# Causal softmax in chunks of 32 queries, its probabilities regrouped through DRAM

## The reference

```
x = _layernorm(x + _L0_attn_ref(x, wq, wk, wv, wo))
x = _layernorm(x + _L0_xattn_ref(x, ctx_4096, weight))
x = _layernorm(x + _L0_ffn_ref(x, A, B, Wr, br))
```

```
scores = jnp.einsum('bhqd,bhkd->bhqk', q, k) / math.sqrt(HEAD_DIM)
causal = k_pos <= q_pos
final = jnp.where(allowed, scores, NEG)
attn = jax.nn.softmax(final, axis=-1)
out = jnp.einsum('bhqk,bhkd->bhqd', attn, v)
```

## Time and profile before

| | |
|---|---|
| median of 3 runs | 1435.54 us |
| profiled execution | 1439.9 us |
| its span | 1438.1 us |
| TensorE busy | 1370.1 us, 95% |
| VectorE busy | 1092.5 us, 76% |
| ScalarE busy | 932.5 us, 65% |
| GpSimd busy | 985.9 us, 69% |
| DMA | 213.03 MB, mean 148 GB/s |

### The profile page before, as it was taken

One profiled execution on the slowest core, in us unless ns is written; L12 is line 12 of the kernel. 1 busy time (PEld: TensorE's weight loads), 2 busy tenths in 40 slices (PEclk: granted clock), 3 DMA queues, 4 the chain that ended last, 5 costly groups with the idle time before them and its releaser, 6 DMA issues. The chain is left out here.

```text
span 1438.1 us, 32297 instructions
## 1 busy us (share of the span) xinstructions
PE 1370.1 (95%) x8288; PEld 1061.4 (74%) x8288; DVE 1092.5 (76%) x3869; ACT 932.5 (65%) x3258; POOL 985.9 (69%) x936
## 2 busy tenths in 40 slices
PE   6899999999999999999985899999999999999995
PEld 4677777777777777777753688888888888888874
DVE  5677777777777777777766477878887788887784
ACT  5678878788787887878765354555554455555542
POOL 3677767777677776777754566777766777776753
PEclk9999999999999999999996899999999999999997
DMA  6345445454454544545465857656666766666751
GB/s 227 113 121 156 122 139 152 119 155 122 141 152 119 152 125 141 151 119 153 125 179 164 218 145 170 165 153 163 159 159 165 175 150 159 165 156 162 157 117 44
DMA packets 108861, 213.03 MB, mean 148 GB/s; under 512 B 26640, under 2 KB 32272, under 8 KB 108816
## 3 DMA queue, kind: packets, MB, share of 16 engines
q1 hardware_dynamic: 108816, 212.51, 54.0%
HBM read 131.83 MB, written 34.47 MB: 116 GB/s over the span
## 5 line engine op out<-in xcount | busy, mean ns | idle before, releaser
L432 PE MATMUL wo_ps<-weights,halves 128*128 128x512 f32 x2304 | 573.8, 400 | 11.9 <-DVE weights L611 11.8
L432 PEld LDWEIGHTS wo_ps<-weights,halves 128*128 128x128 f32 x2304 | 423.8, 189 | 129.3 <-issue 34.3
L694 ACT ACTIVATE pexp<-sm,smin 128x128 f32<-128x128 f32 x1024 | 398.7, 393 | 119.1 <-DVE smin L562 118.4
L1039 PE MATMUL wo_ps<-weights,halves 128*128 128x512 f32 x1488 | 401.1, 402 | 2.0 <-DVE yz L1142 2.0
L811 POOL TENSOR_TENSOR pn<-pexp,prec 128x512 f32<-128x512 f32 x256 | 267.8, 1046 | 151.6 <-DVE prec L569 151.5
L1392 POOL TENSOR_TENSOR prods<-prod,prods 128x512 fp32r<-128x512 f32 x192 | 259.9, 1362 | 134.0 <-ACT prods L1286 129.1
L1039 PEld LDWEIGHTS wo_ps<-weights,halves 128*128 128x128 f32 x1488 | 273.4, 190 | 61.2 <-issue 3.7
L562 DVE CUSTOM_DVE_ANT_0 sm<-s_ps,mask_t 128x128 f32<-128x128 f32 x1024 | 231.8, 281 | 80.0 <-PE s_ps L462 80.0
L1286 ACT CAST prods<-prod 128x512 fp32r<-128x512 f32 x192 | 118.8, 621 | 165.9 <-DVE prod L1176 129.4
L1176 DVE TENSOR_TENSOR prod<-att,x 128x512 f32<-128x512 f32 x192 | 186.2, 985 | 14.0 <-DMA att<-sim_scratch 11.1
L694 ACT ACTIVATION_READ_ACCUMULATOR pexp<-sm,smin 128x1 f32 x1024 | 194.8, 190 | 0.0
(11 more groups left out here) (99 smaller groups left out, 1668.6 us busy)
## 6 DMA issues: line engine op xcount, KB each, us to landing
att<-sim_scratch SPq DMA_DIRECT2D x192, 252.0 KB
pt<-blocks SPq DMA_DIRECT2D x640, 64.0 KB, 2.0
ctx_t<-in_ctx SPq DMA_DIRECT2D x32, 576.0 KB, 4.5
raw<-in_xT SPq DMA_DIRECT2D x32, 512.0 KB, 3.7
raw<-ot_scratch SPq DMA_DIRECT2D x32, 512.0 KB, 6.6
xn<-in_x SPq DMA_DIRECT2D x32, 512.0 KB, 7.2
out<-late SPq DMA_DIRECT2D x32, 512.0 KB, 6.2
ot_scratch<-ot SPq DMA_DIRECT2D x63, 256.0 KB, 2.1
```

Of the source, the lines that this page charges most:

```text
L432: mm = pe.matmul(qkv_ps[(par + g) % 2][:], xs[:, par, xl, k], w_sb[:, wl, g, k], start=(k == 0 and n == 0), stop=(k == KT - 1 and n == 2))
L694: ins = nc.scalar.activation(pexp[:, c % 2, i * P:(i + 1) * P], sm[:, c % 2, i * P:(i + 1) * P], ACT.Exp, bias=smin[:, c % 2, i:i + 1], sc ...
L1039: mm = pe.matmul(wo_ps[n][:], os_t[:, par, ol, k], wo_sb[:, wl, k, n * BANK:(n + 1) * BANK], start=(k == 0 and m == 0), stop=(k == KT - 1 ...
```

## The change

A chunk is no longer one query head with all 128 queries. It is one block of 32 queries (`tb`, in the order 3, 2, 1, 0) of all four query heads, again with 128 rows on the partitions. A query in block `tb` sees at most the first w = 32 (tb+1) keys, so masking, exponential, scaling and transposing run over w of 128 keys for each key head: 128, 96, 64, 32 in the four chunks of a group. The scores of a chunk are computed for these keys only. The copy of the transposed queries out of PSUM (`copy_q`) reorders them so that the 32 queries of four heads lie together.

After the transpose a block has the four heads of the query block on its free side but the wrong partition order: partitions are (head, key in block). A copy between partitions of SBUF could not regroup them by whole 32-partition blocks, so they pass through a scratch tensor in DRAM. `send_p` writes the blocks of a group with two DMAs, first those of the query blocks 3 and 2 (all four key blocks, 512 KB), then those of 1 and 0 (two key blocks, 256 KB). `fetch_p` waits for both writes and reads with four DMAs, one for each key block kb, of 256, 192, 128 and 64 KB. `pt` is laid out with the head outside and the query block inside.

```diff
+TB = (3, 2, 1, 0)
...
+    p_dram = nc.dram_tensor("p_scratch", [2, NU, P, QB, QB, NI, SB], F32, kind="Internal").ap()
...
-    blocks = sb("blocks", [P, NU, QB, NJ, NI, SB])
-    pt = sb("pt", [P, NU, QB, NJ, NI, SB])
+    blocks = sb("blocks", [P, NU, QB, QB, NI, SB])
+    pt = sb("pt", [P, NU, NJ, QB, NI, SB])
...
-    MOVES = 16 * QB * (QB + 1) // 2
+    MOVES = 16 * QB
+    SENT = 16 * 2
...
+    def chunk(c):
+
+        u, j = divmod(c, NC // NU)
+        return u, TB[j], (TB[j] + 1) * SB
...
-        def move_p(a, u):
+        def send_p(a, par, u):
+
+            for part, keys, rows in ((0, slice(0, QB), slice(2, QB)), (1, slice(0, 2), slice(0, 2))):
+                wait(sp, turned, after(a, NC, NJ * u + 2 * part + 2))
+                sp.dma_start(p_dram[par, u, :, keys, rows], blocks[:, u, keys, rows]).then_inc(p_out[u], 16)
+
+        def fetch_p(a, par, u):
...
-            wait(sp, turned, after(a, NC, NJ * (u + 1)))
             wait(sp, pv_done, after(a - 1, NU, u + 1))
-            for qb in range(QB):
-                for kb in range(qb + 1):
-                    sp.dma_start(pt[kb * SB:(kb + 1) * SB, u, qb], blocks[qb * SB:(qb + 1) * SB, u, kb]
-                                 ).then_inc(p_in[u], 16)
+            wait(sp, p_out[u], after(a, SENT, SENT))
+            for kb in range(QB):
+                src = p_dram[par, u, :, kb, kb:].rearrange("(j k) b i q -> k j b i q", j=NJ)
+                sp.dma_start(pt[kb * SB:(kb + 1) * SB, u, :, kb:], src).then_inc(p_in[u], 16)
...
-                move_p(b, 1)
+                send_p(b, par, 1)
+                fetch_p(b, par, 1)
...
-                move_p(a, 0)
+                send_p(a, 1 - par, 0)
+                fetch_p(a, 1 - par, 0)
...
-            for j in range(NJ):
+            for c in range(u * NJ, (u + 1) * NJ):
+                _, tb, w = chunk(c)
                 for i in range(NI):
                     rows = slice(i * DH, (i + 1) * DH)
-                    mm = pe.matmul(s_ps[i][:, j * P:(j + 1) * P], qt[rows, u, j * P:(j + 1) * P],
-                                   kt[rows, par, u * P:(u + 1) * P], start=True, stop=True,
+                    mm = pe.matmul(s_ps[i][:, tb * P:tb * P + w], qt[rows, u, tb * P:(tb + 1) * P],
+                                   kt[rows, par, u * P:u * P + w], start=True, stop=True,
                                    tile_position=(i * DH, 0))
...
-                ins = dve.tensor_tensor_reduce(sm[:, c % 2, i * P:(i + 1) * P], s_ps[i][:, j * P:(j + 1) * P],
-                                               mask_t[:], 1.0, 3e38, ALU.add, ALU.min, smin[:, c % 2, i:i + 1])
+                ins = dve.tensor_tensor_reduce(sm[:, c % 2, i * P:i * P + w], s_ps[i][:, tb * P:tb * P + w],
+                                               mask_t[:, P - w:P], 1.0, 3e38, ALU.add, ALU.min, smin[:, c % 2, i:i + 1])
...
-            nc.scalar.copy(qt[:, u], turn_ps[:]).then_inc(qt_in, 1)
+            nc.scalar.copy(qt[:, u].rearrange("p (b j q) -> p j b q", b=QB, j=NJ),
+                           turn_ps[:].rearrange("p (j b q) -> p j b q", j=NJ, b=QB)).then_inc(qt_in, 1)
...
-                ins = nc.scalar.activation(pexp[:, c % 2, i * P:(i + 1) * P], sm[:, c % 2, i * P:(i + 1) * P],
+                ins = nc.scalar.activation(pexp[:, c % 2, i * P:i * P + w], sm[:, c % 2, i * P:i * P + w],
```

31 lines of the change are left out of this document (17 added, 14 removed).

## The result

The changed kernel takes 1453.41 us (median of 4 runs, 1452.34 to 1459.26) against 1435.65 us for the kernel before. The ratio on record, from the single runs, is 1.0133, 95% interval 1.0119 to 1.0147 (the quotient of the two medians is 1.0124). The forecast was 1431.0 us and faster. The sign was wrong; the time lies at the edge of the range (1426 to 1454).

What follows compares the result with a forecast made beforehand. TensorE was taken to bound the steady stretch, busy for 652.66 of 653.00 us. Scores -4.8, start -0.3 and end +0.5 summed to -4.6 us, so 1431.0 us was forecast, range 1426 to 1454.

Steps and rivals of the forecast that it cites:

- TensorE: Score blocks: only the uncovered last stream shortens, by 0.080 us a block, from 1.10 to 1.02; -4.8 us in all.
- B: Score blocks: the gap after the last stream is fixed, so the block stays at 1.10 us; 1435.7 us, chance 0.15.
- C: Score blocks: streams set the pace, saving 18.6 us in place of 4.6, block 0.79 us; 1417 us, chance 0.07.
- Softmax engines: ScalarE, VectorE, GpSimd in the steady steps: shorter instructions, but they already wait for TensorE; costed at nothing.
- The way of the probabilities: Transfer through DRAM before the weighings: u=1 lands at 414.9, TensorE asks at 416.06; slack 1.2 us, cost nothing.
- upper bound: Way of the probabilities: writes at half rate and landing at 3.7 us give 418.4, a 2.3 us stall every step.
- lower bound: Way of the probabilities: the last read landed at 413.9, cost nothing.
- Rival A: u=1 weighing in each of 29 steps: probabilities come late, 1 us stall gives 1460 us, 2.3 gives 1498; chance 0.20.
- The page's surcharge: Writes to DRAM: 2 us extra for HBM under high load would land reads at 416.9 and stall each step; not adopted.
- The end: Last weighings of the first part: transfer latency is on the path, last read landed at 782.6 against 782.1; +0.5 us.
- start: Before the score block at 50.66: TensorE's wait shrinks through shorter exponentials; -0.3 us, bounds 0 and -1.2.

Runs made afterwards that it cites:

- e1: The changed kernel with SP issuing the next item's context load behind the u=1 reads of the probabilities, not ahead of their writes: 1438.3 us.
- e5: e1 with the score chunks of a group issued in rising width (32 to 128 columns): 1443.6 us, ratio 1.0063.
- e4: The kernel before with only its ten copies of the probabilities replaced by two writes to DRAM and four reads of whole blocks: 1475.2 us.
- e2: The changed kernel with each write of the probabilities cut to 64 KB, and reads of unchanged size taken from a DRAM input: 1428.6 us.
- e8: e1 with the last matrix step's two round trips overlapped and a 512 KB load moved behind the first half's writes: 1435.2 us.
- e9: The changed kernel with the four writes of a step issued from ScalarE's queue between its exponentials instead of from SP: 1432.2 us.
- e12: e9 with ScalarE's last two writes put ahead of its work on part 2's last weight block and a root: 1431.0 us.
- e6: The changed kernel with the second weighing of a step moved three projections later in TensorE's order: 1479.5 us.

## Why the prediction was wrong

**TensorE: right.** The block fell from 1.10 to 1.02 us, and where nothing stalls the 29 steps take 647.94 us (e1) against a forecast of 652.99 less 4.64, 648.35. e5 gives the 4.64 back by the order of the chunks alone. Rivals B and C are refuted. One count in the prediction is off and changes nothing: 58 blocks are 1856 records, and the 1888 of the earlier trace rows are 59 blocks, since its window reaches to 717 us.

**Softmax engines: right.** Their instructions became shorter and their waits longer. They did give one thing that I had counted but not priced: in the changed kernel the last transpose of u=1 is 0.28 us instead of 0.68. e4, which lacks this and the early first write, loses 20.0 us to the probabilities in 28 steps where the changed kernel loses 9.2 in 14.

**The way of the probabilities: this is the step that failed, a term put at nothing.** From the start of the scores of u=0, in the stalled step shown above and as the median of the 29 steps:

| | forecast | step shown | median |
|---|---|---|---|
| context landed | +7.4 (408.3) | +8.8 | +7.9 |
| writes landed | +9.6 (410.5) | +10.9 | +10.0 |
| last read issued | +11.6 | +12.3 | +11.4 |
| last read landed | +14.0 | +16.0 | +15.2 |
| TensorE asks | +15.2 | +15.1 | +15.1 |

The forecast had 1.2 us of slack. The largest term that was wrong is the landing of the last read: 3.8 us by the median (3.7 to 4.3 in the 29 steps) in place of 2.4, which alone is more than the slack. I took it next to a store's 2.1 us, although the row for a load from DRAM said 3.7. The issues of the reads, 0.44 us each instead of 0.62, gave some 0.6 back.

The second wrong term is where the line starts. The writes behind the context were sized right: they land 2.0 us after it in each of the 29 steps (1.95 to 2.10), where I had 2.2. But the context itself took 4.5 to 7.6 us to land, 6.3 in the step shown, where I had 4.6, the median of before. It decides which steps wait: in the 14 that wait it landed at +7.9 to +10.0 us, in the other 15 at +7.0 to +8.0. My line began at the context; the input's 512 KB and the last read of u=0 were still in flight when it was issued (they landed at 410.87 and 409.10, the context was issued at 407.89), while in the step of before the last copy of u=0 had landed at 402.85, ahead of the context's issue at 403.73. That these bytes are what delays the context is argued from the trace: in e2, where the writes of both halves are small, the context took 3.8 us, but no run changes the bytes ahead of it alone. My upper bound held the reads' 3.7 us, and I called it the unlikely end. The lower bound, 413.9, does not follow from the terms beside it, which give 414.5; it cost nothing either way.

Rival A was the right mechanism at its own threshold: it decides when the way from the last transpose to the landing passes 10.5 us. In the stalled step the last transpose ended at 409.97 and TensorE was released 11.5 us later. It does not do so in every step, as A had it: 14 of the steps wait, by 1.5 us at most, and between them lie steps of 22.3 us that don't wait. TensorE's own delay may give the transfers of the next step a head start; that is not shown, and twice three steps in a row wait (from 110 and from 405 us). The loss is 0.4 us a step on average (11.5 us over 29), not A's 1 us.

**The page's surcharge.** The prediction took its 2 us from "DMA: Bandwidth & Descriptors" of the Trainium skill. The section "Anatomy of one DMA" gives its fixed 2 us for transfers that GpSimd issues, and this kernel's come from SP and ScalarE; the 2 us of a loaded HBM stand in the section "Latency and other measured facts". A 64 KB write into DRAM lands in 2.0 us (e2), no later than a copy of 64 KB inside SBUF before, so the trace shows no surcharge for the write. The sum with the extra 2 us came to 416.9, that is +16.0: what the stalled step shows, and 0.8 more than the median. It was near in time and wrong in place, since the excess sits in the reads and in the context ahead of the writes; that it was near is in part luck. Here the rule that spoke against the change deserved more than the chance of 0.20.

**The end: the mechanism right, the size off.** I wrote +0.5 us, bounds -1.9 and +3; it was +4.9. From the end of the 29 steps (715.90 before, 723.93 after):

| | forecast | measured |
|---|---|---|
| first half's writes landed | +54.6 | +55.0 |
| second half's writes issued | +59.1 | +59.0 |
| second half's writes landed | +62.3 | +65.9 |
| last read issued | +64.3 | +67.2 |
| last read landed | +66.7 | +71.0 |

Both round trips were in the sum, and the second one left when I said. Its writes then landed 3.6 us late: I had 2.23 MB moved in 6.3 us at 353 GB/s, the rate of the busiest 2 us before, and they took 10.8 us at 206 GB/s. The reads' landing adds 1.4 us as in the steady steps, and their faster issue gives 0.6 back. e8, e9, e12 and e2 (71.2, 67.7, 65.9 and 65.0 us) show that the last round trip and its bytes set the end's length: the next stage begins 3.9 us after the last weighing in each of them.

**Sum.** Steady: +6.5 us instead of -4.8. That is 11.5 us more than e1: 9.2 us of waits for the probabilities, 0.5 for the copied queries, and 1.6 by which TensorE was busy for longer (649.57 against 647.94), which no run explains. e1 removes them together. End: +4.9 instead of +0.5. e12 is 4.6 us below before (1431.04 against 1435.60 on the same chip). That this equals the forecast's gain is luck: in its trace the steady stretch is 3.3 us shorter than before and the end 4.2, the latter by an order of ScalarE's and SP's work that the forecast didn't have. The range of the prediction also starts lower than its own terms: the best end and start give 1427.7, not 1426.

Open are whether a second queue, at the same issue times and with the same bytes ahead, shortens a landing; and what the regrouping would cost inside SBUF. The section on the change says that copies inside SBUF could not do it by whole blocks of 32 partitions. By the indices of `fetch_p` they could: the 32 partitions of one head and one key block go to 32 whole partitions of `pt`, 16 copies for each group. With one transfer in place of two this is the nearest rival to the way through DRAM, and nobody ran it.

## What to carry to other kernels

A route that replaces a transfer by two dependent ones is priced by what is in flight ahead of each, back to transfers issued ahead of the one where the sum begins, by the rate that a whole train of transfers gets, and by the landing time of its own kind in the trace, not by the best 2 us of a window or by a store's landing for a load. Put such transfers ahead of bulk loads that have slack, and give them to an engine whose list has no other long wait. And where every engine waits for the next in a ring, slack added at one edge is taken from another: follow the queue of the issuing engine before moving an instruction.

## What the runs showed of the hardware

- Reads from DRAM of 64 to 256 KB land in 3.6 to 4.1 us by the median, whatever their size and whoever wrote the data (e1, e2, e4, e9), single ones up to 5.7 us (after); writes of 64 KB into DRAM in 2.0 (e2).
- Writes of 256 KB took 3.2 us (medians of e1 and e9), 4.0 (median of after), and single ones 6.2 (e12) and 7.6 (after, at the end), with more in flight.
- Two writes of 768 KB together, queued behind a load of 576 KB, landed 1.95 to 2.10 us after it in all 29 steps (after); it was the load's own landing that varied, from 4.5 to 7.6 us.
- Four issues of DMAs on SP take 1.75 us, 0.44 each, where the ten before took 0.62 each.
- ScalarE can issue four DMAs a step between its exponentials without a cost that shows: TensorE's waits for the copied queries are 0.4 us in e9, 0.5 in the changed kernel.
- With 20 waits of TensorE ahead of its scores, 29.5 us in all, the mean granted clock of the steady stretch was 0.98 (e6); with 14 ahead of the weighings, 9.2 us in all, it was 1.00 (after).
